# A routed expert kernel: the capacity search spread over twelve tiles with its steps as numbers, and the list scatters five a tile for eight tiles

## The chip, the cores and the metric

The kernel runs on one core of one Trainium2 chip. The metric is the device time of one execution in microseconds (us). TensorE multiplies matrices, VectorE, ScalarE and GpSimd compute, SyncE issues loads and stores; each of them works through its own list of instructions in order and waits on semaphores for the others. GpSimd also issues the indirect DMAs (scatters and gathers by a list of row numbers).

## The reference

One layer: image patches are embedded and joined with text tokens (32 sequences of 274 tokens, 192 wide), then attention with 12 heads, then a layer of experts with two sets of four experts each. The change is in the routing of the experts. What matters of it, cut down:

```python
N = h.shape[0]                      # 8768 tokens
capacity = int(N / 4)               # 2192 tokens for each common expert
pc = softmax(h @ Wsc + bsc); pmax_c = max(pc); route_c = argmax(pc)
dropped = rank of the token by -pmax_c among those of its expert >= capacity
common = sum over e of (route_c == e) * ffn(h, W1c[e], b1c[e], W2c[e], b2c[e])
pu = softmax(h @ Wsu + bsu);        route_u = argmax(pu)
unique = sum over e of (route_u == e) * ffn(h, W1u[e], b1u[e], W2u[e], b2u[e])
out = common + dropped * unique     # unique only where the common expert dropped the token
```

`ffn` is 192 to 768, GELU, back to 192.

## The kernel before, in words

The attention part ends near 830 us. It has written each token's row to `rows_d`, and GpSimd has scattered the rows into `sorted_d`, ordered by common expert. The expert part then works on tiles of 256 rows of one expert. The first 35 (`FIXED`) are common ones, read from `sorted_d`. The later ones belong to the unique experts: their rows are found by lists in `list_d`, which can be made only once it is known which tokens are dropped. Tiles 0 to 43 are written out one by one, the rest sit in a loop that stops at the last tile in use.

Each engine runs `body(t)` for the tiles in turn. For tile t:

- SyncE loads weights and rows four tiles ahead into one of four buffers (`load_w`, `load_sorted`): the big part of the weights at L1547, the rows at L1560, the rest of the weights at L1550. It does so once Y of tile t-4 is done, and for the rows also once GpSimd has read that tile's row numbers out of the buffer (`sid_ready`, waited for at L1558).
- TensorE (`up`, `turn`, `down`): 30 up products for tile t (L1790), four transposes of tile t+1's rows (L1772, L1773), 24 down products of tile t-1 in two halves (L1801).
- ScalarE: GELU for the six blocks of tile t, and rounded copies (`Wh`, `XH`) of the next tile's weights and rows.
- VectorE: the differences `Wl` (L1947, two halves) and `XL`, `XH` (L1938, L1940) of the next tile; then bias (`Yb`, L1957) and sum (`Y`, L1971) of tile t-1.
- GpSimd (a turn of its body): the two row scatters of Y of tile t-3 (`send`, L1690), the copy of tile t-2's row numbers (`number`, the cast `sid` at L1662), and the list scatters where there are any (`send_ids`, L184).

**The search.** A common expert drops the tokens whose `pmax` lies under a threshold. The threshold T of each of the four experts is found by bisection in 26 tests. `test` (VectorE) adds the step to T (`cand`, L1983), compares all keys with it (`flag`, L1984) and sums over a partition (`part`, L1985). `count` (TensorE, L1814) sums over partitions. `take` (VectorE) turns the count into 0 or the step (`gain`, L1989), halves the step (L1990) and adds the gain to T (L1991). The first two (`LEAD`) run ahead of tile 0, where the kernel still waits for loads. The others are spread over the tiles so that each count stands between TensorE's products: `SEARCH` tiles with `TESTS` tests each. `done` makes VectorE wait for each of its own results before the next instruction.

**After it.** `ties` runs in tile `TIES`, `drops` in `DROPS`, `drop_flags` in the next one, `unique_rows` in `PLACE` (it sets `ranked`), `unique_tiles` and `unique_turns` in the two after (which set `placed`; SyncE waits for that in tile `EARLY` = 22). From tile `SPREAD` on GpSimd scatters the 72 columns of token numbers into the lists, so many a tile as the table `BEFORE` says, until tile 31.

**The barrier.** In tile 32 SyncE waits for all of the list scatters before it loads the first list, and everything that it loads afterwards, the weights and rows of tile 33 first, is queued behind this wait:

```python
if t.number == FIXED - AHEAD:
    sp.wait_ge(spread_out, 16 * COLS)
if t.number is not None and FIXED <= t.number + AHEAD < STATIC:
    load_list(...)
```

In the trace this wait is shown at L1571.

Of the kernel before, what the change touches and what calls it, by code (L numbers as in the profile page):

```python
# [10 lines left out]
ALU = mybir.AluOpType  # L11
# [3 lines left out]
P = 128  # L15
# [20 lines left out]
CAP = N // NX  # L36
# [6 lines left out]
FIXED = -(-N // ROWS)  # L43
# [1363 lines left out]
UNITS = GROUP * (NG - 1)  # L1407
AHEAD = 3
STATIC = (-(-CT // DEPTH) + 1) * DEPTH
LEAD, SEARCH, TESTS = 2, 8, 3  # L1410
LOWEST = 0.25 - 2.0 ** -10
TIES, DROPS, PLACE = SEARCH, SEARCH + 1, SEARCH + 3
SPREAD = PLACE + 1
BEFORE = [sum(4 if n < SPREAD + 12 else 3 for n in range(SPREAD, t)) for t in range(FIXED - 2)]
assert (FIXED, CT, STATIC) == (35, 38, 44)
assert LEAD + SEARCH * TESTS >= 26 and BEFORE[-1] >= COLS

# [21 lines left out]
def experts(nc, block, sem, H, A, K, rows_d, sorted_d, list_d, out):  # L1439

    ctx = ExitStack()
    with ctx:
# [9 lines left out]
        C, eye, OH, key = K.c, K.ident, K.OH, K.key  # L1452
        T = sb("T", [P, NX])
        cand = sb("cand", [P, NX])
        step = sb("step", [P, 1])
        gain = sb("gain", [P, NX])
        part = sb("part", [P, NX])
        need = sb("need", [P, NX])
# [302 lines left out]
        def _(pe):  # L1761
# [54 lines left out]
            def body(t):  # L1816
                searching = t.number is not None and t.number < SEARCH
                if t.opens:
                    turn(t)
                up(t)  # L1820
                if searching:
                    count(LEAD + TESTS * t.n)
                if not t.closes:
                    turn(t.next())
                if not t.opens:
                    down(t.before(1), 0)
                if searching:
                    count(LEAD + TESTS * t.n + 1)
                if not t.opens:
                    down(t.before(1), 1)  # L1830
                if searching:
                    count(LEAD + TESTS * t.n + 2)
                if t.number == DROPS:
                    count(LEAD + TESTS * SEARCH)
                    ranks(0, tie96[:].rearrange("p e c -> p (e c)"), NX * FLAT)
                if t.number == DROPS + 1:
                    ranks(1, OH[:, 1].rearrange("p e c -> p (e c)"), NX * COLS)
# [54 lines left out]
        def _(dve):  # L1892
# [21 lines left out]
                done(dve.tensor_tensor_scan(first[:, 0:ne], C["one"][:, 0:ne], K.nt[:, 0:ne], 0.0, ALU.mult, ALU.add))  # L1914

            dve.wait_ge(H.left, 1)
            for x, value in ((T, LOWEST), (step, 0.5)):
                done(dve.memset(x[:], value))

            def by_batch(x):  # L1920
                return x.rearrange("p e (b k) -> p (e b) k", k=3)
# [56 lines left out]
                add_bias(t)  # L1978
                add_rest(t)

            def test():

                done(dve.tensor_scalar(cand[:], T[:], step[:, 0:1], None, ALU.add))  # L1983
                done(dve.tensor_tensor(flag[:], key[:], by_e(cand[:]), ALU.is_ge))  # L1984
                dve.tensor_reduce(part[:], flag[:], AX.X, ALU.add).then_inc(part_ready, 1)  # L1985

            def take(k):
                dve.wait_ge(counted, k + 1)
                done(dve.tensor_scalar(gain[:], cnt_ps, float(CAP), step[:, 0:1], ALU.is_ge, ALU.mult))  # L1989
                dve.tensor_scalar(step[:], step[:], 0.5, None, ALU.mult)  # L1990
                done(dve.tensor_tensor(T[:], T[:], gain[:], ALU.add))  # L1991

            def ties():
# [72 lines left out]
            def body(t):  # L2066
                searching = t.number is not None and t.number < SEARCH
                if t.opens:
                    split(t, 0)
                    split(t, 1)  # L2070
                    turned(t)
                if t.number is not None and 0 < t.number <= SEARCH:
                    take(LEAD + TESTS * t.n - 1)
                if searching:
                    test()
                if not t.closes:
                    split(t.next(), 0)
                if searching:
                    take(LEAD + TESTS * t.n)
                    test()  # L2080
                if t.number == DROPS + 1:
                    drop_flags()
                if t.number == PLACE:
                    unique_rows()
                if t.number == PLACE + 1:
                    unique_tiles()
                if t.number == PLACE + 2:
                    unique_turns()
                if not t.closes:
                    turned(t.next())  # L2090
                if searching:
                    take(LEAD + TESTS * t.n + 1)
                    test()
                if not t.closes:
                    split(t.next(), 1)
                if not t.opens:
                    add_bias(t.before(1))
                    if not t.before(1).based():
                        add_rest(t.before(1))
                    if t.number in (FIXED + 1, CT, CT + 2):  # L2100
                        add_rest(static({FIXED + 1: FIXED, CT: CT - 2, CT + 2: CT - 1}[t.number]))
                    if t.number in (CT + 4, CT + 5):
                        add_rest(static(2 * t.number - CT - 8))
                        add_rest(static(2 * t.number - CT - 7))
                if t.number == TIES:
                    ties()
                if t.number == DROPS:
                    drops()
                if t.number == PLACE:
                    unique_counts()  # L2110

            for k in range(LEAD):
                test()
                take(k)
            tiles(dve, body, load_last, finish)

# [92 lines left out]
```

## Time and profile before

| | |
|---|---|
| median of three runs | 1244.79 us (1237.87 to 1248.96) |
| the profiled execution | 1241.2 us, its span 1239.3 us |
| busy in the span | TensorE 1145.1 us (92%), VectorE 858.9 (69%), ScalarE 607.8 (49%), GpSimd 726.8 (59%) |
| mean granted clock of TensorE | 0.958 of full speed |

The span is what the trace covers, the 1.9 us beside it lie around it. Times in the rows below count from the span's start. A granted clock of 1.00 is TensorE's higher level of 2.4 GHz, 0.50 the lower of 1.2 GHz. The expert part runs from 833 us to the end; the shares of the whole span say little on it, so the rows go by stretch, by tile and by engine. In a line of the timeline the number in brackets is the time in which the engine sat idle before it, and behind the arrow stands what ended it; "issue" is time in which it waited for nothing that the trace shows.

### The profile page before, as it was taken

How to read it: one execution, taken by the hardware profiler on the slowest of the kernel's cores; microseconds unless marked ns; L12 is line 12 of the kernel's file. 1: busy time of each engine (PE TensorE's matmuls, PEld its weight loads, DVE VectorE, ACT ScalarE, POOL GpSimd, SP SyncE). 2: the span in 40 equal slices, each digit the busy share in tenths (PEclk: the TensorE clock that was granted, in tenths of full speed). 3: DMA queues.
4: the chain of work that ended last, by engine and by line, in shares of the span. 5: the costliest groups of instructions: out<-in, count | busy, mean ns of one | idle time of the engine just before them, and what ended most of it. 6: DMA issues, size and time to landing. Idle time of an engine off the chain costs nothing. (4 is left out here: it accounts for less than half of the span.)

```text
span 1239.3 us, 33362 instructions
## 1 busy us (share of the span) xinstructions
PE 1145.1 (92%) x12686; PEld 988.4 (80%) x12686; DVE 858.9 (69%) x1933; ACT 607.8 (49%) x1088; POOL 726.8 (59%) x1126
## 2 busy tenths in 40 slices
PE   4889999999999999999999998737999999999993
PEld 3667888888888788788788786527999999999993
DVE  6557777788788788788788787456988655555341
ACT  2135555555555555555555545414545555555540
POOL 6235555555765765765765763553633877755575
PEclk9879999999999999999999999767999999999997
DMA  6001112113323323322422312258876888978651
GB/s 217 18 23 58 50 43 73 59 44 103 112 69 94 117 74 88 122 75 77 127 81 75 120 65 63 98 164 321 295 261 207 263 270 268 289 223 291 217 179 33
DMA packets 84514, 168.08 MB, mean 136 GB/s; under 512 B 16590, under 2 KB 57845, under 8 KB 84352
## 3 DMA queue, kind: packets, MB, share of 16 engines
q1 hardware_dynamic: 70688, 139.90, 35.8%
q0 software_dynamic: 13664, 26.00, 5.9%
q8 instruction: 104, 1.70, 0.6%
q14 instruction: 58, 0.48, 0.1%
HBM read 123.85 MB, written 45.45 MB: 137 GB/s over the span
## 5 line engine op out<-in xcount | busy, mean ns | idle before, releaser
L811 ACT ACTIVATE PT<-round_banks 128x1752 f32<-128x1752 f32 x96 | 156.7, 1632 | 110.4 <-PE round_banks L632 110.4
L1880 ACT ACTIVATE Gl<-h_ps,W 128x256 f32<-128x256 f32 x264 | 115.9, 474 | 169.6 <-PE h_ps L1790 161.2
L958 POOL TENSOR_SCALAR_AFFINE_SELECT PT<-PT 128x512 f32<-128x512 f32 x192 | 118.3, 643 | 114.6 <-ACT PT L811 114.1
L1801 PE MATMUL y_ps<-W,Gl 128*128 128x192 f32 x1056 | 181.2, 325 | 0.0
L1801 PEld LDWEIGHTS y_ps<-W,Gl 128*128 128x128 f32 x1056 | 171.3, 189 | 0.0
L1790 PE MATMUL h_ps<-XH,Wh 128*128 128x256 f32 x528 | 147.5, 297 | 6.8 <-issue 2.6
L1790 PE MATMUL h_ps<-XH,Wl 128*128 128x256 f32 x528 | 140.2, 287 | 0.0
L1084 DVE TENSOR_TENSOR capped<-round_banks,masks_f 128x1024 f32<-128x1024 f32 x96 | 117.3, 1222 | 31.6 <-PE round_banks L605 31.6
L533 PE MATMUL gen<-w_emb,xh 128*128 128x192 f32 (+1 forms) x768 | 125.1, 270 | 14.0 <-POOL xl L898 13.7
L1690 POOL DMA_INDIRECT out_dram<-Y,sid x76 | 79.6, 1048 | 77.7 <-DVE Y L1971 56.7
L1947 DVE TENSOR_TENSOR Wl<-W,Wh 128x768 fp32r<-128x768 f32 x88 | 84.3, 959 | 56.8 <-ACT Wh L1860 54.3
L533 PEld LDWEIGHTS gen<-w_emb,xh 128*128 128x128 f32 (+1 forms) x768 | 102.9, 168 | 19.8 <-issue 15.4
L632 PEld LDWEIGHTS round_banks<-QKT 32*128 32x128 f32 x2304 | 95.2, 188 | 27.8 <-issue 14.5
L1088 DVE TENSOR_REDUCE nm<-capped 128x8 f32<-128x1024 f32 x96 | 116.0, 1208 | 0.0
L632 PE MATMUL round_banks<-QKT 32*128 32x146 f32 (+2 forms) x2304 | 110.0, 319 | 5.3 <-DMA QKT<-mT 2.4
L1790 PEld LDWEIGHTS h_ps<-XH,Wh 128*128 128x128 f32 x528 | 103.2, 195 | 8.5 <-DVE Wl L1947 5.8
L918 POOL TENSOR_SCALAR veps<-mv 128x2 f32<-128x2 f32 (+1 forms) x80 | 18.0, 225 | 151.8 <-DVE mv L1096 150.5
L1790 PEld LDWEIGHTS h_ps<-XH,Wl 128*128 128x128 f32 x528 | 103.2, 196 | 0.0
L533 PE MATMUL gen<-w_emb,xl 128*69 128x192 f32 (+1 forms) x384 | 101.8, 265 | 0.0
L605 PEld LDWEIGHTS round_banks<-QKT 32*128 32x128 f32 x1536 | 71.4, 189 | 37.2 <-issue 26.7
L235 POOL DMA_INDIRECT sorted_d<-stage,pos x72 | 74.3, 1032 | 41.2 <-DMA stage<-rows_d 19.8
L605 PE MATMUL round_banks<-QKT 32*128 32x256 f32 (+1 forms) x1536 | 92.7, 356 | 5.5 <-ACT PT L811 5.3
(287 smaller groups left out, 2662.0 us busy)
## 6 DMA issues: line engine op xcount, KB each, us to landing
W<-in_experts_dram SPq DMA_DIRECT2D x44, 771.0 KB, 5.4
W<-in_experts_dram SPq DMA_DIRECT2D x44, 672.0 KB
xT<-in_xT_dram SPq DMA_DIRECT2D x32, 591.0 KB, 4.8
X<-sorted_d SPq DMA_DIRECT2D x35, 386.0 KB, 5.7
stage<-rows_d SPq DMA_DIRECT2D x64, 192.0 KB
rows_d<-h SPq DMA_DIRECT2D x32, 192.0 KB, 3.9
out_dram<-h SPq DMA_DIRECT2D x32, 192.0 KB, 6.5
rows_d<-xn SPq DMA_DIRECT2D x32, 192.0 KB, 2.1
```

The source lines that it names most:

```text
L533: mm = pe.matmul(g[0:m, 0:D], x[:, c, cols], w_emb[:, c, part_of_w, :], start=(c == 0 and n == 0), stop=(c == EC - 1 and n == 2))
L605: mm = pe.matmul(R[:, i, at:at + (k + 1) * P], q[rows, j, tok(k)], q[rows, JG + j, 0:(k + 1) * P], start=True, stop=True, skip_group_check ...
L632: mm = pe.matmul(R[:, i, at:at + n], q[rows, JG + j, klo:klo + P], q[rows, j, qlo:qlo + n], start=True, stop=True, skip_group_check=True)
L811: act.activation(PT[(JG * b + j) % 2][:], R[:, :, 0:438], ACT.Exp, scale=SCALE).then_inc(exps, 1)
L958: pool.affine_select(x[:, :, at:at + P], x[:, :, at:at + P], [[0, GH], [1, P]], ALU.is_ge, 0.0, base=0, channel_multiplier=-1)
L1084: dve.tensor_tensor(capped[:], blocks[:, :, 0:3:2, :], masks[:].rearrange("p (a b k) -> p a b k", a=1, b=1).broadcast_to([P, GH, 2, P]), A ...
L1088: dve.tensor_reduce(x[:, :, 0:3:2], capped[:], AX.X, ALU.max, negate=True).then_inc(capped_read, 1)
L1690: pool.indirect_dma_start(out_rows, bass.IndirectOffsetOnAxis(target(t)[:, k:k + 1], 0), Y[t.i][:, k, :], None, bounds_check=N - 1, oob_is ...
L1790: mm = pe.matmul(h_ps[f % 3][:, 0:ROWS], w[t.par][:, cols], x, start=(k == 0), stop=(k == len(products) - 1))
L1801: mm = pe.matmul(y_ps[t.par][:, k * D:(k + 1) * D], Gl[t.par][:, f, k * P:(k + 1) * P], W[t.i][:, W2O + f * D:W2O + (f + 1) * D], start=(f ...
L1880: act.activation(Gl[t.par][:, f, :], h_ps[f % 3][:, 0:ROWS], ACT.Gelu, bias=W[t.i][:, B1O + f:B1O + f + 1]).then_inc(g_ready, 1)
L1947: dve.tensor_tensor(halves(Wl[t.par], half), halves(W[t.i], half), halves(Wh[t.par], half), ALU.subtract).then_inc(wl_ready, 1)
```

## The change

The search takes twelve tiles with two tests each in place of eight with three. The step of each test is written into the instructions as a number (a power of a half), so the tile `step`, its memset and its halving (L1990) are gone, and `cand` and `gain` have no second input of a column. All that follows the search moves four tiles on, by the names that are set from `SEARCH`: the ties from tile 8 to 12, the drops from 9 to 13, `unique_rows` from 11 to 15. The list scatters start in tile 16 in place of 12; they were four a tile for twelve tiles and three for eight, and are now five a tile for eight tiles and four for eight.

```diff
-LEAD, SEARCH, TESTS = 2, 8, 3
+LEAD, SEARCH, TESTS = 2, 12, 2
-BEFORE = [sum(4 if n < SPREAD + 12 else 3 for n in range(SPREAD, t)) for t in range(FIXED - 2)]
+BEFORE = [sum(5 if n < SPREAD + 8 else 4 for n in range(SPREAD, t)) for t in range(FIXED - 2)]
...
-        step = sb("step", [P, 1])
...
-                if searching:
-                    count(LEAD + TESTS * t.n + 2)
...
-            for x, value in ((T, LOWEST), (step, 0.5)):
-                done(dve.memset(x[:], value))
+            done(dve.memset(T[:], LOWEST))
...
-            def test():
-
-                done(dve.tensor_scalar(cand[:], T[:], step[:, 0:1], None, ALU.add))
+            def test(k):
+
+
+                done(dve.tensor_scalar(cand[:], T[:], 0.5 ** (k + 1), None, ALU.add))
...
-                done(dve.tensor_scalar(gain[:], cnt_ps, float(CAP), step[:, 0:1], ALU.is_ge, ALU.mult))
-                dve.tensor_scalar(step[:], step[:], 0.5, None, ALU.mult)
+                done(dve.tensor_scalar(gain[:], cnt_ps, float(CAP), 0.5 ** (k + 1), ALU.is_ge, ALU.mult))
...
                 if searching:
-                    test()
+                    test(LEAD + TESTS * t.n)
...
                     take(LEAD + TESTS * t.n)
-                    test()
+                    test(LEAD + TESTS * t.n + 1)
...
-                if searching:
-                    take(LEAD + TESTS * t.n + 1)
-                    test()
```

How it moves instructions, at two places. On VectorE in one search tile, from the test before the first half of `Wl` to the next tile's bias, before:

```order
L1983 TENSOR_SCALAR cand<-T,step 128x4
L1984 TENSOR_TENSOR flag<-key,cand 128x288
L1985 TENSOR_REDUCE part<-flag 128x4
L1947 TENSOR_TENSOR Wl<-W,Wh 128x2x384
...
L1938 TENSOR_TENSOR XL<-xt_ps,XH 128x256
L1940 TENSOR_TENSOR XH<-xt_ps,XH 64x256
L1989 TENSOR_SCALAR gain<-in_col_ps,step 128x4
L1990 TENSOR_SCALAR step<-step 128x1
L1991 TENSOR_TENSOR T<-T,gain 128x4
L1983 TENSOR_SCALAR cand<-T,step 128x4
L1984 TENSOR_TENSOR flag<-key,cand 128x288
L1985 TENSOR_REDUCE part<-flag 128x4
L1947 TENSOR_TENSOR Wl<-W,Wh 128x2x384
```

And now:

```order
L1980 TENSOR_SCALAR cand<-T 128x4
L1981 TENSOR_TENSOR flag<-key,cand 128x288
L1982 TENSOR_REDUCE part<-flag 128x4
L1943 TENSOR_TENSOR Wl<-W,Wh 128x2x384
L1986 TENSOR_SCALAR gain<-in_col_ps 128x4
L1987 TENSOR_TENSOR T<-T,gain 128x4
L1980 TENSOR_SCALAR cand<-T 128x4
L1981 TENSOR_TENSOR flag<-key,cand 128x288
L1982 TENSOR_REDUCE part<-flag 128x4
L1934 TENSOR_TENSOR XL<-xt_ps,XH 128x256
L1936 TENSOR_TENSOR XH<-xt_ps,XH 64x256
L1943 TENSOR_TENSOR Wl<-W,Wh 128x2x384
```

The take and the test between `XH` and the second half of `Wl` are gone, and the halving of the step with every other take. On GpSimd where the lists are scattered, the turns of tiles 23 and 24 before, each with two row scatters (of `Y`, to the rows in `sid`), a cast and its lists:

```order
L1690 DMA out_0_dram<-Y0,sid0 8768x192 x2
L1662 CAST sid1<-X1 128x2
L184 DMA list_d<-meta,pos 39168x2 x4
L1690 DMA out_0_dram<-Y1,sid1 8768x192 x2
L1662 CAST sid2<-X2 128x2
L184 DMA list_d<-meta,pos 39168x2 x3
```

The same turns now:

```order
L1689 DMA out_0_dram<-Y0,sid0 8768x192 x2
L1661 CAST sid1<-X1 128x2
L184 DMA list_d<-meta,pos 39168x2 x5
L1689 DMA out_0_dram<-Y1,sid1 8768x192 x2
L1661 CAST sid2<-X2 128x2
L184 DMA list_d<-meta,pos 39168x2 x4
```

Each turn from tile 16 to 31 has one list scatter more than it had, the turns of tiles 12 to 15 have none.

## Rows read from the trace of the kernel before

**Rows 1.** Busy time by stretch, us; x counts instructions, PEclk is the granted clock.

```profile
core 0: us, PE busy (x) PEld busy (x) DVE busy (x) ACT busy (x) POOL busy (x), PEclk, DMA share, GB/s
852.00:854.00 2.00, 0.48 (x3) 0.48 (x3) 1.90 (x6) 0.00 (x0) 0.00 (x0) 0.50 0.99 402
858.00:860.00 2.00, 2.00 (x18) 2.00 (x18) 1.12 (x2) 1.88 (x5) 0.40 (x1) 0.93 0.64 215
910.25:919.29 9.04, 8.96 (x66) 8.52 (x66) 8.47 (x26) 4.58 (x9) 2.76 (x3) 1.00 0.67 229
972.39:980.33 7.94, 7.94 (x60) 7.94 (x60) 4.14 (x8) 4.51 (x9) 6.41 (x7) 1.00 0.91 260
1051.80:1115.36 63.56, 63.56 (x466) 63.56 (x466) 32.66 (x56) 36.13 (x72) 42.27 (x50) 1.00 0.83 261
```

**Rows 2.** Waits of SyncE's queue from 860 to 1140: us, times, longest.

```profile
SPq L1571 <- DMA list_d<-meta,pos: 8.1, 1, 8.1
SPq L1559 <- POOL sid L1662: 1.6, 1, 1.6
```

**Rows 3.** Timeline at the list barrier: start, us, engine, instruction.

```profile
1113.95 0.34 SPq L1547 DMA_DIRECT2D W<-in_experts_dram  x1
1119.56 0.33 PE L1772 MATMUL xt_ps<-ident,X 128*128 128x128 f32 x1 [0.31 <-DMA X<-sorted_d]
```

**Rows 4.** Timeline of VectorE in tiles 0, 7 and 10.

```profile
851.28 0.43 DVE L1940 TENSOR_TENSOR XH<-xt_ps,XH 64x256 fp32r<-64x256 f32 x1
917.27 0.22 DVE L1989 TENSOR_SCALAR gain<-in_col_ps,step 128x4 f32<-128x4 f32 x1
917.78 0.23 DVE L1983 TENSOR_SCALAR cand<-T,step 128x4 f32<-128x4 f32 x1
918.54 0.45 DVE L1985 TENSOR_REDUCE part<-flag 128x4 f32<-128x288 f32 x1
937.05 0.16 DVE L2007 TENSOR_SCALAR need<-in_col_ps 128x4 f32<-128x4 f32 x1
```

**Rows 5.** Timeline of TensorE in tiles 0, 1, 4 and 7.

```profile
853.52 0.59 PE L1814 MATMUL in_col_ps<-part,ones 128*128 128x4 f32 x2 [2.14 <-DVE part L1985]
853.97 0.56 PE L1790 MATMUL h_ps<-XH,Wh 128*128 128x256 f32 x1
891.94 0.39 PE L1814 MATMUL in_col_ps<-part,ones 128*128 128x4 f32 x2
916.77 2.21 PE L1801 MATMUL y_ps<-W,Gl 128*128 128x192 f32 x12
919.05 0.39 PE L1814 MATMUL in_col_ps<-part,ones 128*128 128x4 f32 x2
```

**Rows 6.** Timeline of SyncE: two loads of sorted rows.

```profile
878.86 0.34 SPq L1560 DMA_DIRECT2D X<-sorted_d  x1
984.02 0.34 SPq L1560 DMA_DIRECT2D X<-sorted_d  x1
```

**Rows 7.** DMA issues from 860 to 900: count, KB each, median us to landing.

```profile
X<-sorted_d SPq DMA_DIRECT2D x4, 386.0 KB, 6.3
```

**Rows 8.** The list scatters: ns min/median/max, first and last start.

```profile
L184 POOL DMA_INDIRECT list_d<-meta,pos x72: 972/975/1708, 955.2 to 1107.7; - x72
```

**Rows 9.** Timeline of GpSimd: turns of tiles 15, 16 and 24.

```profile
977.86 0.98 POOL L1690 DMA_INDIRECT out_dram<-Y,sid  x1 [0.30 <-issue]
980.48 0.98 POOL L184 DMA_INDIRECT list_d<-meta,pos  x1 [0.16 <-POOL sid L1662]
985.80 0.97 POOL L1690 DMA_INDIRECT out_dram<-Y,sid  x1 [0.30 <-issue]
1049.35 0.97 POOL L1690 DMA_INDIRECT out_dram<-Y,sid  x1 [0.31 <-issue]
```

**Rows 10.** Timeline of VectorE and GpSimd where a list scatter is longest.

```profile
964.43 0.96 DVE L1947 TENSOR_TENSOR Wl<-W,Wh 128x768 fp32r<-128x768 f32 x1
964.53 1.71 POOL L184 DMA_INDIRECT list_d<-meta,pos  x1 [0.30 <-issue]
```

More of the change, by code:

```diff
@@ L2112, in _ @@
             for k in range(LEAD):
-                test()
+                test(k)
                 take(k)
```

## The prediction

> **What bounds the kernel now.** I read the busy time by stretch first [rows 1]. The change touches only the expert part, from 833 us on. In the tile from 972.39 to 980.33 and again from 1051.80 to 1115.36 TensorE is busy in all of the stretch at a granted clock of 1.00: an expert tile costs TensorE 7.94 us, and nothing else sets the pace. Two kinds of stretch differ. A search tile (910.25 to 919.29) takes 9.04 us, and VectorE is busy 8.47 of them. At the start of the part TensorE does little: 0.48 of 2 us from 852 to 854, with its clock at 0.50.
>
> Then the waits of SyncE's queue: it stood 8.1 us at L1571 until the last list scatter had landed [rows 2]. That looks harmless, since TensorE waited only 0.31 us for the rows that SyncE loads behind this barrier (tile 33's transposes at 1119.56 [rows 3]). But a wait above zero means that the barrier has no slack left: whatever makes the last list scatter later makes the end later. So GpSimd's chain of scatters has to be timed beside TensorE's tiles.
>
> **Part 1, the search.** In a search tile VectorE takes a count (gain 0.22 us, with the step's and T's updates the next test starts 0.51 after it at 917.78), and makes the next test, whose part takes 0.45 and ends at 918.99, three times [rows 4]. A take and a test are 1.7 us, from 917.27. On TensorE the third count started at 919.05, after down products that began at 916.77 and, 12 at 0.158 (a tile's 24 take 3.78), would have ended at 918.66: 0.39 us of waiting, and 0.24 until the next tile started at 919.29 [rows 1, 5]. With two tests a tile VectorE has 9.04 - 1.7 = 7.3 us to do. Steps as numbers save more: L2007, two numbers on the same PSUM tile, took 0.16 where gain took 0.22 [rows 4]; with as much on cand and 0.07 for the step's own multiply, 0.2 a test, it is 6.9 us. That is under TensorE's 7.94, so TensorE sets the search tiles: 7.94 + two counts of 0.14 to 0.24 = 8.3 us (8.45 if the second test is late by 0.15).
>
> Tiles 5 to 7 gain 3 x (9.04 - 8.3) = 2.2 us. Tiles 8 to 11 now carry two counts each, 4 x 0.35 = 1.4 us lost. The tie, drop and place steps keep their price, four tiles later, and `placed` still comes before tile 22, where SyncE asks for it.
>
> At the start, the third test of tile 0 held TensorE: 2.14 us idle ahead of its count, and tile 1 started at 853.97 [rows 5]. Without it tile 1 starts when XH ends, at 851.7 [rows 4], 2.2 us earlier, perhaps at the higher clock too. It won't keep this: tile 5's rows were issued only at 878.86 [rows 6], 1.6 us behind their time for a sid cast on GpSimd [rows 2], and the search doesn't move that cast, which stands behind the last staged scatters. They take 6.3 us to land in this stretch [rows 7], until 885.2; transposes, down products and a count take 4.45 more; tile 5 starts at 889.6. Today the count ahead of it begins at 891.94 [rows 5], so it starts at 892.3: 2.7 us won, between 1.5 (rows land later) and 5 (they are not waited for).
>
> Part 1 alone: 2.7 + 2.2 - 1.4 = **3.5 us faster**, if GpSimd keeps up. What VectorE loses besides is hidden by TensorE's tile; that cover is 1 us.
>
> **Part 2, the list scatters.** The 72 of them started from 955.2 to 1107.7, 0.975 us each with 0.30 before the next [rows 8, 9]. A turn of GpSimd at four lists is two row scatters and the sid cast (977.86 to 980.48, 2.62 us) and 4 x 1.28 for the lists: 7.74 us; the next began at 985.80. From 977.86 to 1049.35 nine turns took 71.49 us, 7.94 each [rows 9]. GpSimd is full there already, with 0.2 us a turn for stretches. At five lists a turn is 9.02 us, 1.1 more than TensorE's tile, and in the last eight tiles four lists (7.74) stand where three did. GpSimd becomes the slowest engine for sixteen tiles.
>
> So I time it as a chain that waits for nobody: 71 list starts after the first (90.9 us) and 15 turns' other work at 2.62 (39.3): 130.2 us. Today 19 turns lie between (140.7 us) and it takes 152.5, with room for 11.8 of waits and stretches. Stretches: a scatter that starts while VectorE's Wl runs gets longer; the longest, 1.71 for 0.98 us, began 0.10 after a Wl of 0.96 [rows 10]. The first stretch of turns, beside the place steps, took 977.86 - 955.20 = 22.66 for 12 lists and two turns' rest (20.6): 2.06 over. Low bound: 2.06 + 13 turns x 0.2 = 4.7 us. High: the longest stretch once a turn, 2.06 + 13 x 0.73 = 11.6. I take 5.5, near the steady turns.
>
> The first list is at 955.2 now, in tile 12; then in tile 16: 955.2 - 2.7 - 2.2 + 4 x 8.3 = 983.5. The last: 983.5 + 130.2 + 5.5 = 1119.2, **11.5 us later** than 1107.7. From the last list to the next weights' issue are 6.28 us (to 1113.95 [rows 3]), and TensorE was already waiting behind those. So the 11.5 go to the end whole, and part 1's gain is inside them, since it only starts the chain earlier. Queued behind the barrier on SyncE are the weights and rows of tile 33 and of all later ones. Before that, late sid casts hold back the rows of tiles 23 to 26: today the cast ends just before 980.48 for rows that are issued at 984.02 [rows 6, 9], 3.5 us of room, gone after three or four turns at 1.1. Those small stalls lie inside the same 11.5.
>
> The long one is in one piece. Tile 32 can start some 12.6 us after turn 30 (cast 2.6, rows 5.7, transposes and down products 4.3), at 1117, and its up products end at 1121; tile 33's rows land at 1119.2 + 6.3 + 5.6 = 1131.1. Ten us idle, and the clock was at 0.50 after far less (852 to 854), and at 0.93 in the stretch from 858 to 860, 4 to 5 us after tile 1 had started [rows 1, 5]. Half speed for 4.3 us costs 2.2 us, between 0 (clock kept) and 2.5. "TensorE: Matmul & The Clock Gate" of the Trainium skill (part "What's actually happening") names the same two levels, 1.2 and 2.4 GHz; by that rule, the trace agrees.
>
> **The sum.** 11.5 + 2.2 = 13.7 us. The profiled execution took 1241.2 us, 1.9 over its span; with 13.7 it is 1254.9. It lies 3.6 under the median of the three runs, 1244.79, which becomes **1258.5**. Bounds: the chain with 4.7, tile 5 at 887.3 and no clock loss, 1116.1 - 1107.7 = 8 us, 1253. The chain with 11.6, tile 5 at 890.8, clock 2.5: 18.8 + 2.5 = 21, 1266.
>
> **Rivals.** (a) GpSimd has room: the 0.30 us ahead of each scatter is put down to issue and not to work, so five might be issued closer. The lists then end in time, only part 1 counts, and the time is 1244.8 - 3.5 = 1241, not slower. It decides from a spacing under 1.12 us (11.5 us less over 71 starts). Against it: nine turns in a row held 1.28. "DMA: Bandwidth & Descriptors" of the Trainium skill (section "Anatomy of one DMA — SWDGE (gpsimd) path") calls descriptor generation small and puts most of the fixed 2 us of a DMA at its completion; by that, a fifth scatter is nearly free to GpSimd and the time is that of (a). The trace doesn't agree: GpSimd is busy 0.97 us with each.
>
> (b) The delay is partly swallowed: after the barrier the loads come closer together, or the last tiles, where VectorE waits for base rows anyway, absorb it. Half stays, some 6 us: 1251. Against it: those waits start from the Y of tiles behind the barrier, which move too. (c) GpSimd is stretched as in the high bound or more, as it no longer runs in step with the tiles: 1266 to 1270. "SBUF — State Buffer" of the Trainium skill (section "Who interferes with whom") says that a VectorE instruction with two SBUF inputs contends with a GpSimd one that reads SBUF, and the first blocks the other; the row at 964.53 agrees.
>
> **How the numbers follow.** The forecast (8 to 17 us slower) has 0.68, (a) 0.12, (b) 0.10, (c) 0.10. Within 1%, 12.4 us, a measurement of this kernel can't tell a change from none. That cuts the forecast in two: 0.38 of its 0.68 lie above, and with (c) slower has 0.48. Faster by over 1% would need three times part 1: 0.03, taken from (a). The rest, 0.49, is within. The range takes in the bounds and most of (b), and leaves out (a) and the far end of (c): 1246 to 1266.
>
> **What would show it.** Search tiles of 8.3 us with VectorE idle in them; gain near 0.16 us; turns of 9.0 to 9.5 us on GpSimd in tiles 17 to 23, none waiting for Y; SyncE waiting for sid casts from tile 23 on; the last list near 1119; TensorE idle some 10 us ahead of tile 33's transposes, a clock of 0.50 behind it. It is wrong if GpSimd still waits for Y in tiles 24 to 31, or if TensorE's wait at tile 33 stays under 1 us.

## The result, and the profile after

The changed kernel takes **1262.99 us** (median of 4 runs, 1256.93 to 1263.42), the kernel before 1241.56 (median of 4, 1237.87 to 1248.96). The ratio is 1.0132 with a 95% interval of 1.0099 to 1.0165: 16.4 us slower, between 12.3 and 20.5. The forecast was 1258.5 and 13.7 us slower.

The profiled execution took 1262.94 us, with a span of 1261.2 against 1239.3 before, 21.9 us more. Not all of that is the change's. The first count on TensorE, with which the expert part begins, stands at 838.39 us here and at 834.03 before, and ahead of it the change touches only VectorE's memset and its first `cand`. Over the twelve kernels profiled for this study, it stands anywhere from 830.24 to 840.97. So below I measure from the first count. From there to the end of the span are **405.3 us before and 422.8 after: 17.5 us more**.

The search did what was expected. First the busy time by stretch, as in [rows 1]: a search tile, the tile-4 wait, and the stretch around tile 33.

```profile
core 0: us, PE busy (x) PEld busy (x) DVE busy (x) ACT busy (x) POOL busy (x), PEclk, DMA share, GB/s
921.00:929.34 8.34, 8.34 (x64) 8.34 (x63) 6.61 (x17) 4.58 (x9) 2.44 (x3) 1.00 0.71 232
877.00:880.00 3.00, 0.26 (x4) 0.17 (x2) 0.00 (x0) 0.00 (x1) 2.33 (x3) 0.96 0.90 295
880.00:883.00 3.00, 1.88 (x8) 1.88 (x9) 1.99 (x6) 2.66 (x6) 2.53 (x4) 0.50 1.01 418
...
1127.00:1131.00 4.00, 1.00 (x9) 0.79 (x7) 0.00 (x0) 0.00 (x0) 2.92 (x3) 1.00 0.08 21
1133.00:1137.00 4.00, 0.00 (x0) 0.00 (x0) 0.71 (x1) 1.58 (x4) 3.09 (x4) 0.50 1.00 322
1137.00:1141.00 4.00, 3.88 (x14) 3.88 (x15) 2.06 (x4) 1.68 (x3) 1.75 (x3) 0.50 1.02 403
```

In the search tile TensorE is busy in all 8.34 us and VectorE in 6.61 of them (8.47 of 9.04 before [rows 1]). A take and a test on VectorE, as in [rows 4]:

```profile
925.86 0.15 DVE L1986 TENSOR_SCALAR gain<-in_col_ps 128x4 f32<-128x4 f32 x1
926.05 0.16 DVE L1987 TENSOR_TENSOR T<-T,gain 128x4 f32<-128x4 f32 x1
926.25 0.17 DVE L1980 TENSOR_SCALAR cand<-T 128x4 f32<-128x4 f32 x1
```

The steps as numbers made gain 0.15 us where it was 0.22, and cand 0.17 where it was 0.23. cand starts 0.39 after gain, not 0.51.

GpSimd and SyncE, as in [rows 2, 8, 9]: the scatters of the lists, one turn of five lists from start to start, and what SyncE's queue waited for from 860 to 1140.

```profile
L184 POOL DMA_INDIRECT list_d<-meta,pos x72: 971/974/1715, 991.0 to 1127.1; - x72
```

```profile
1008.50 0.97 POOL L1689 DMA_INDIRECT out_dram<-Y,sid  x1 [0.30 <-issue]
...
1011.11 0.98 POOL L184 DMA_INDIRECT list_d<-meta,pos  x1 [0.16 <-POOL sid L1661]
...
1017.72 0.97 POOL L1689 DMA_INDIRECT out_dram<-Y,sid  x1 [0.30 <-issue]
```

```profile
SPq L1558 <- POOL sid L1661: 54.0, 14, 5.7
SPq L1570 <- DMA list_d<-meta,pos: 12.3, 1, 12.3
```

The turn takes 9.22 us, against TensorE's tile of 7.94; after a first one of 10.6 beside the place steps, six turns of five lists took 9.0 to 9.6. The 72 lists run in 136.1 us without a wait for `Y`. SyncE now stands at the sid cast in 14 tiles (one before), for up to 5.7 us, and 12.3 us at the barrier.

What it ends in, as in [rows 3]: SyncE's first loads behind the barrier, and TensorE at tile 33.

```profile
1131.05 0.34 SPq L1546 DMA_DIRECT2D W<-in_experts_dram  x1
1132.15 0.34 SPq L1559 DMA_DIRECT2D X<-sorted_d  x1
...
1137.12 0.48 PE L1771 MATMUL xt_ps<-ident,X 128*128 128x128 f32 x1 [9.13 <-DMA X<-sorted_d]
```

TensorE waits **9.13 us** where it waited 0.31 before. The transpose itself takes 0.48 and not 0.27 to 0.33, since the clock is at 0.50. From there to the next `Yb` on VectorE, the sum that follows a tile's down products and so marks the start of the next tile, are 7.33 us, 4.68 before.

The chain of waits runs straight through this. Its pieces from 1124 us on:

```profile
1124.52 0.97 POOL list_d L184
1125.80 0.99 POOL list_d L184
1127.09 2.09 DMA list_d<-meta,pos
1132.15 4.93 DMA X<-sorted_d
1137.12 0.48 PE xt_ps L1771
1138.24 6.10 PE y_ps L1800 x24
```

Ahead of the barrier it is GpSimd that stands on the chain. In a stretch that TensorE bounds there would be rows of `h_ps` and `y_ps`.

One thing went otherwise than predicted, at the start. TensorE in tile 4:

```profile
881.12 0.47 PE L1771 MATMUL xt_ps<-ident,X 128*128 128x128 f32 x1 [3.86 <-DMA X<-sorted_d]
```

It arrived earlier than before, waited 3.86 us for tile 4's rows, and the clock fell to 0.50 (the row of 880 to 883 above). Before, there was no wait there:

```profile
877.50 0.31 PE L1772 MATMUL xt_ps<-ident,X 128*128 128x128 f32 x1
```

**Where the 17.5 us are.** I follow the starts of the tiles (by their `Yb`) and the last list, each from its kernel's first count. At tile 5 the changed kernel is 0.2 us ahead, at tile 18 0.1. The last list comes at 288.7 instead of 273.6: 15.1 later. From there to the landing of tile 33's rows are 10.03 us (1137.12 - 1127.09) instead of 11.89: 1.9 won. From the transposes to `Yb` are 2.65 more, the clock. What follows takes 116.7 us instead of 115.1: 1.6 more. Together 15.1 - 1.9 + 2.65 + 1.6 = 17.5. The last term is within what this stretch varies by: it took from 112.6 to 118.7 us in eleven of the twelve kernels profiled (in fill4_barrier33 a wait for rows lies inside it).

### The profile page after: what moved, and what is told of

The parts are those of the page before. It is cut to its first block and busy times, and to the rows that moved or that the text cites. A ratio compares the mean times of both kernels' runs of the same rounds, so it can differ in the third digit from the quotient of the medians.

```text
span 1261.2 us, 33335 instructions
## 1 busy us (share of the span) xinstructions
PE 1152.9 (91%) x12686; PEld 997.3 (79%) x12686; DVE 853.7 (68%) x1906; ACT 608.2 (48%) x1088; POOL 727.7 (58%) x1126
## 5 line engine op out<-in xcount | busy, mean ns | idle before, releaser
L1800 PE MATMUL y_ps<-W,Gl 128*128 128x192 f32 x1056 | 186.3, 331 | 0.0
L1800 PEld LDWEIGHTS y_ps<-W,Gl 128*128 128x128 f32 x1056 | 175.6, 193 | 0.0
L533 PE MATMUL gen<-w_emb,xh 128*128 128x192 f32 (+1 forms) x768 | 128.2, 275 | 14.0 <-POOL xl L898 13.7
L550 PE MATMUL gen<-w_qkv,xnT 97*128 97x200 f32 (+1 forms) x256 | 96.8, 461 | 1.6 <-ACT xnT L789 1.6
```

The lines of the kernel that those rows point to most:

```text
L533: mm = pe.matmul(g[0:m, 0:D], x[:, c, cols], w_emb[:, c, part_of_w, :], start=(c == 0 and n == 0), stop=(c == EC - 1 and n == 2))
L550: pe.matmul(o, xTs[:, 0, tok(k)], w[0:KC + 1, 0, cols], start=True, stop=False)
L1800: mm = pe.matmul(y_ps[t.par][:, k * D:(k + 1) * D], Gl[t.par][:, f, k * P:(k + 1) * P], W[t.i][:, W2O + f * D:W2O + (f + 1) * D], start=(f ...
```

## The experiments

All ratios are against the kernel before, run beside it on the same chip. "Profiled" is the time of the one profiled execution; in some kernels it lies far from the median, and what is read from its rows need not hold for the others. "Part" is the time from the first count to the end of the span, "last list" the start of the last list scatter from the first count, both of that execution; "tile 4" and "barrier" are what TensorE waited for rows there, us.

| kernel | median us | profiled | ratio (95%) | part | last list | tile 4 | barrier |
|---|---|---|---|---|---|---|---|
| before | - | 1241.20 | 1 | 405.3 | 273.6 | - | 0.31 |
| after | 1262.99 | 1262.94 | 1.0132 (1.0099 to 1.0165) | 422.8 | 288.7 | 3.86 | 9.13 |
| steps_only | 1240.61 | 1240.35 | 0.9976 (0.9945 to 1.0006) | 404.4 | 271.5 | 0.49 | 0.34 |
| late_lists | 1258.46 | 1254.78 | 1.012 (1.008 to 1.0161) | 422.3 | 288.5 | - | 9.17 |
| half_lists | 1240.55 | 1234.90 | 0.9971 (0.9943 to 1.0) | 400.7 | 269.8 | 2.68 | - |
| barrier33 | 1246.88 | 1240.11 | 1.003 (1.0003 to 1.0058) | 408.1 | 286.8 | 3.13 | - |
| lead4 | 1249.07 | 1250.66 | 1.0064 (1.004 to 1.0088) | 407.8 | 279.7 | 1.19 | 6.87 |
| filled_wait | 1258.23 | 1247.96 | 1.014 (1.0108 to 1.0173) | 415.8 | 288.7 | 3.79 | 0.17 |
| lead6_barrier33 | 1240.62 | 1239.85 | 0.9993 (0.9964 to 1.0021) | 407.7 | 276.7 | - | - |
| steps_barrier33 | 1240.09 | 1242.42 | 0.9972 (0.9946 to 0.9997) | 402.6 | 271.3 | - | - |
| fill4_barrier33 | 1246.87 | 1254.16 | 1.0021 (0.9985 to 1.0058) | 415.4 | 286.0 | 0.82 | 4.25 |
| lead4_barrier33 | 1240.97 | 1240.18 | 0.9962 (0.9931 to 0.9994) | 404.4 | 282.5 | 3.25 | 0.57 |

**steps_only**: the kernel before, with three tests a tile and its lists where they were, and only the steps written as numbers.

```diff
-                done(dve.tensor_scalar(cand[:], T[:], step[:, 0:1], None, ALU.add))
+                done(dve.tensor_scalar(cand[:], T[:], 0.5 ** (k + 1), None, ALU.add))
...
-                done(dve.tensor_scalar(gain[:], cnt_ps, float(CAP), step[:, 0:1], ALU.is_ge, ALU.mult))
-                dve.tensor_scalar(step[:], step[:], 0.5, None, ALU.mult)
+                done(dve.tensor_scalar(gain[:], cnt_ps, float(CAP), 0.5 ** (k + 1), ALU.is_ge, ALU.mult))
```

> The kernel before with the steps as numbers alone; search of eight tiles with three tests, lists as before. Theory 1 (list chain and barrier make the loss): a search tile falls from 9.04 to about 8.6 us on VectorE, some 0.45 us in each of eight tiles, so 3 to 4 us faster than before if the list chain keeps its room; the last list stays about 152 us behind the first. Theory 2 (the searching tiles themselves carry the loss, whatever GpSimd does): nothing of it is in this kernel, also 0 to 4 us faster. What it tells: the size of this part alone.

Search tiles take 8.45 to 8.58 us instead of 8.90 to 9.04, with all three tests in them, and the last list comes 2.1 us earlier. In the part 0.9 us is left of it. The ratio's interval takes in 1: a gain of up to 7 us or none. So most of what the cheaper search brings needs neither fewer tests a tile nor later lists: three tests with numbers cost 8.5 us, two cost 8.34.

**late_lists**: the kernel before, with its own search, and the changed kernel's plan for the lists alone.

```diff
-SPREAD = PLACE + 1
-BEFORE = [sum(4 if n < SPREAD + 12 else 3 for n in range(SPREAD, t)) for t in range(FIXED - 2)]
+SPREAD = PLACE + 5
+BEFORE = [sum(5 if n < SPREAD + 8 else 4 for n in range(SPREAD, t)) for t in range(FIXED - 2)]
```

> The kernel before with its search as it was, and only the list scatters moved: they start in tile 16 and go five a tile for eight tiles and four for eight. Theory 1: first list near 985, last 135.5 to 136 us behind it, near 1121, 13 us later than before; TensorE idle 9 to 10 us ahead of tile 33's transposes, clock 0.50 behind it; 13 to 16 us slower than before. Theory 2: as fast as before.

This is the whole loss by itself: 1.012 against the change's 1.0132, and a part of 422.3 against 422.8. The lists of late_lists, and TensorE at tile 33:

```profile
L184 POOL DMA_INDIRECT list_d<-meta,pos x72: 971/972/1578, 984.0 to 1119.1; - x72
```

```profile
1129.23 0.48 PE L1772 MATMUL xt_ps<-ident,X 128*128 128x128 f32 x1 [9.17 <-DMA X<-sorted_d]
```

They are in the same place from the first count as in the changed kernel (288.5 and 288.7), although this kernel's search is the slow one: the first list comes 0.7 us later here, the chain behind it is 0.9 shorter. So the changed kernel's search is worth next to nothing there. In this execution tile 5 started 1.5 us later than before (60.2 from the first count, not 58.7): at the end of tile 3 TensorE waited 2.02 us for a `part` (0.82 before), and in tile 4 the clock stood at 0.50 for 3.4 us. Without that the lists would presumably have ended a little earlier.

**half_lists**: the changed kernel with only 36 of the 72 list scatters; the other half of the lists is left out, and the late tiles gather fewer rows.

```diff
-                        sp.wait_ge(spread_out, 16 * COLS)
+                        sp.wait_ge(spread_out, 16 * COLS // 2)
...
-                    for c in range(min(BEFORE[t.number], COLS), min(BEFORE[t.number + 1], COLS)):
+                    for c in range(min(BEFORE[t.number] // 2, COLS // 2), min(BEFORE[t.number + 1] // 2, COLS // 2)):
```

> The changed kernel with only 36 of the 72 list scatters (the other half of the lists stays empty, so the late tiles gather fewer rows), search of twelve tiles with two tests. Theory 1: no turn of GpSimd is longer than a tile, no wait of TensorE at tile 33; the search costs nothing or little against before: between 4 us faster and 3 us slower. Theory 2: 10 to 16 us slower than before, like the changed kernel.

With turns that have room, the last list comes at 269.8, TensorE waits for nothing at the barrier, and the time is 0.9971 of before. That is some 20 us under the changed kernel's. All of its loss needs GpSimd to be full: where its turns have room, the later start of the lists costs nothing. The fewer rows of the late tiles could help too, but the stretch from tile 33 to the end took 113.4 us here, inside what the kernels with all lists show.

**barrier33**: the changed kernel, with SyncE's wait for the last list, and the list loads behind it, one tile later.

```diff
-                    if t.number == FIXED - AHEAD:
+                    if t.number == FIXED - AHEAD + 1:
 
                         sp.wait_ge(spread_out, 16 * COLS)
-                    if t.number is not None and FIXED <= t.number + AHEAD < STATIC:
-                        load_list(Tile((t.number + AHEAD) // DEPTH, (t.number + AHEAD) % DEPTH))
+                    if t.number is not None and FIXED <= t.number + AHEAD - 1 < STATIC:
+                        load_list(Tile((t.number + AHEAD - 1) // DEPTH, (t.number + AHEAD - 1) % DEPTH))
```

> The changed kernel with the wait for the list scatters, and every list load, one tile later on SyncE, behind the loads of tile 33. The same work. Theory 1: tile 33's weights and rows no longer stand behind the barrier, those of tile 34 do; the last list lands as late as before, but TensorE waits 1 to 3 us in place of 9 and keeps its clock: 8 to 11 us faster than the changed kernel, 3 to 8 us slower than the kernel before. Theory 2: no change against the changed kernel, 16 us slower than before.

The lists end nearly as late as in the change (286.8 for 288.7), yet the part is 408.1 and the ratio 1.003: about four fifths of the loss are gone by one position of one wait. (This part is that of the fastest of twelve executions; by the ratios 0.0132 falls to 0.003.) What SyncE's queue waited for in this kernel, from 860 to 1140:

```profile
SPq L1558 <- POOL sid L1661: 50.4, 16, 5.8
...
SPq L1570 <- DMA list_d<-meta,pos: 5.2, 1, 5.2
```

The waits for sid casts are all still there, and cost little beyond two tiles (`Yb` 9.65 and 12.40 us apart there, 6.2 above two normal tiles). The 3.7 us that this part is longer than that of steps_only are within that.

**lead4**: four tests ahead of the tiles, eleven search tiles; so lists one tile earlier, five a tile in four tiles and then four.

```diff
-LEAD, SEARCH, TESTS = 2, 12, 2
+LEAD, SEARCH, TESTS = 4, 11, 2
...
-BEFORE = [sum(5 if n < SPREAD + 8 else 4 for n in range(SPREAD, t)) for t in range(FIXED - 2)]
+BEFORE = [sum(5 if n < SPREAD + 4 else 4 for n in range(SPREAD, t)) for t in range(FIXED - 2)]
```

> The changed kernel with four tests ahead of tile 0 and eleven search tiles of two, so the lists start in tile 15 and go five a tile for four tiles and four for thirteen. Lengths are counted from the first count on TensorE to the end of the span, since the part before differs from one execution to the next (405.3 us for the kernel before, 422.8 for the changed one). Theory 1 (the chain of 71 list starts at 1.28 and the other work of each turn at 2.62, plus some 5.5 us, runs from the first list to the last and then to the barrier): first list 8.3 us earlier than in the changed kernel, one turn more in the chain, so the last is 5.5 to 6 us earlier and the part 416 to 418 us. The two more tests ahead of tile 0 cost nothing, since TensorE waits there for rows, and again ahead of tile 4. Theory 2 (what counts is the number of lists in a turn, four or five): with only four turns of five, nearly all of the loss is gone, 407 to 410.

The last list comes 9.0 us earlier than in the change (5.5 to 6 were expected), and the ratio falls from 1.0132 to 1.0064, some 8 us. The chain itself is as theory 1 has it, 138.3 us for 136.1 and one turn more of 2.6. The part, 407.8, is where theory 2 had it, but the lists are only 9.0 of its 15.0: 0.7 are the rows landing sooner behind the last list, 1.1 the clock, and 4.1 the stretch behind tile 33, which varies as much from kernel to kernel without any such cause. There is a second thing in the start. TensorE at tile 4, and the clock around it, in lead4:

```profile
883.43 0.33 PE L1771 MATMUL xt_ps<-ident,X 128*128 128x128 f32 x1 [1.19 <-DMA X<-sorted_d]
```

```profile
core 0: us, PE busy (x) PEld busy (x) DVE busy (x) ACT busy (x) POOL busy (x), PEclk, DMA share, GB/s
...
880.00:883.00 3.00, 2.24 (x20) 2.15 (x18) 1.24 (x4) 1.20 (x3) 2.08 (x4) 1.00 0.99 336
883.00:886.00 3.00, 2.57 (x18) 2.47 (x18) 2.47 (x7) 2.67 (x6) 2.53 (x4) 1.00 1.00 407
```

Tile 4's rows land 42.5 us after the first count, as in the change (42.7). But the tiles ahead of it began two tests later, so TensorE waits 1.19 and not 3.86, and the clock stays at 1.00. Tile 5 starts at 55.7 from the first count here, at 58.5 in the change, at 58.7 before. The kernel that started its tiles later reached tile 5 first.

**filled_wait**: the changed kernel with eleven products of constants added on TensorE ahead of tile 33's transposes.

```diff
+                if t.number == FIXED - AHEAD:
+                    for _ in range(11):
+                        pe.matmul(in_col[:, 0:NX * FLAT], K.before[:], tie96[:].rearrange("p e c -> p (e c)"), start=True, stop=True)
```

> The changed kernel with eleven products of 128x384 on TensorE (results not used) between tile 32's up products and the transposes of tile 33, about 8.3 us in the 9.1 us that it waits there. Theory 1: the clock stays at 1.00 over the wait, tile 31's down products take 3.9 us in place of 6.1, and the kernel is 2 to 2.5 us faster than the changed kernel (part of 420 to 421 us). If the clock costs nothing on the path, or the products are late themselves: no change or slower.

TensorE in filled_wait, from the added products on:

```profile
1121.39 7.26 PE L1824 MATMUL in_col_ps<-tie,before 128*128 128x384 f32 x22
1128.81 0.33 PE L1771 MATMUL xt_ps<-ident,X 128*128 128x128 f32 x1 [0.17 <-DMA X<-sorted_d]
```

The rows land 9.73 us after the last list (10.03 in the change), so the products only fill the wait, and the clock stays at 1.00. From transposes to `Yb` are 4.69 us, as before the change (4.68), not 7.33. So the clock's share is 2.65 us. The ratio (1.014) doesn't show it: its interval and the change's lie on each other. By time this experiment is inconclusive, by its rows it is not. Its part of 415.8 is no measure either: the profiled execution was the fastest of six, 10.3 us under their median, and 4.1 us of the difference to the change lie behind tile 33.

**lead6_barrier33** and **steps_barrier33**: six tests ahead, ten search tiles and four lists a tile, and the later barrier; and the kernel before with steps as numbers and the later barrier. Their edits beyond those shown:

```diff
-LEAD, SEARCH, TESTS = 2, 12, 2
+LEAD, SEARCH, TESTS = 6, 10, 2
...
-BEFORE = [sum(5 if n < SPREAD + 8 else 4 for n in range(SPREAD, t)) for t in range(FIXED - 2)]
+BEFORE = [sum(4 for n in range(SPREAD, t)) for t in range(FIXED - 2)]
```

> Six tests ahead of tile 0, ten search tiles of two, lists four a tile in tiles 14 to 31, and the list barrier behind tile 33's loads. Theory 1: first list 14 to 17 us earlier than in the changed kernel; no turn of GpSimd longer than a tile, the last list 12 us earlier than in the changed kernel and no wait of note ahead of tiles 33 and 34. Part of 400 to 403 us, 2 to 5 us faster than the kernel before. If the four more tests ahead of tile 0 are not hidden (9 us of them against 4.4 us of waiting at tile 0 and 3.9 at tile 4), 1 to 4 us of that are lost. Theory 2: the barrier's place doesn't matter and the early tests count in full: slower than before by 3 us or more.

> The kernel before with the steps as numbers and the list barrier behind tile 33's loads, search and lists else as before. Theory 1: the part falls from 404.4 (steps as numbers alone) by the 0.5 us that tile 33 waited, to some 404 us: 1 us faster than before. A gain of 3 us or more would show that the barrier cost more than its own wait.

Neither waits at tile 4 or at the barrier. lead6_barrier33 keeps four lists a tile, and SyncE waits 0.9 us in all for sid casts (54.0 in the change). But with its four more tests ahead of the tiles it reaches tile 5 at 59.0, no sooner than the kernel before (58.7), and the time is that of before: 0.9993. Its part, 407.7 where 400 to 403 were expected, also has the longest stretch behind tile 33, 118.7 us. steps_barrier33 has the shortest median, 0.9972 (0.9946 to 0.9997), and can't be told from steps_only: with the lists as before the barrier had no cost to be taken away.

**fill4_barrier33**: barrier33 with 26 added transposes of constants ahead of tile 4's.

```diff
+                if t.number == 4:
+                    pe.wait_ge(xt_ready, t.n)
+                    for _ in range(26):
+                        pe.transpose(xt_ps[:, 0:P], K.before[:], eye[:])
```

> The changed kernel with the list barrier one tile later, and with 26 added transposes of constants (128x128, the same form as the tile's own) on TensorE ahead of tile 4's transposes, written where the real ones overwrite them. They stand in the 3.1 us in which TensorE waited for tile 4's rows; nothing is left out. Theory 1, the start's gain is lost to the clock that falls while TensorE waits for tile 4's rows: at full clock the fillers take some 2.9 us, the wait behind them is under 0.5, the clock stays at 1.00 from there on, and the interval of the base rows' sums over tile 4 goes from 13.0 to some 10.3 us; the part is some 2.7 us shorter than with the late barrier alone (408.1 from the first count), the time 1244. Rival, the rows' landing alone sets tile 5, whatever the clock does: the interval stays near 13, the time 1247.

TensorE at tile 4 in fill4_barrier33:

```profile
875.34 3.04 PE L1766 MATMUL xt_ps<-ident,before 128*128 128x128 f32 x26
879.20 0.33 PE L1775 MATMUL xt_ps<-ident,X 128*128 128x128 f32 x1 [0.82 <-DMA X<-sorted_d]
```

The rows land at 42.25 from the first count, about as ever (42.7 in the change), and the clock stays at 1.00. From transposes to `Yb` are 4.9 us, where they are 7.5 in the change, in filled_wait and in lead4_barrier33. Tile 5 starts at 55.5, 3.2 earlier than before the change and 3.1 earlier than in it: 2.6 the clock, the rest the rows. So the clock does bear on tile 5, and the rival, that the rows' landing alone sets it, falls. The time didn't follow: 1246.87, as with the late barrier alone (1246.88). Against that kernel tile 5 starts only 0.9 us sooner (56.4 there), too little for these times to show. In the profiled execution, the slowest of eleven at 1254.16, it was lost again by a wait for the barrier in tile 34:

```profile
1136.02 0.47 PE L1775 MATMUL xt_ps<-ident,X 128*128 128x128 f32 x1 [4.25 <-DMA X<-sorted_d]
```

Whether the executions near the median wait there too isn't shown. In this one the step from the last list to the next weights' issue took 6.14 us, in barrier33 4.70.

The interval of 10.3 us that I expected was 12.29. I had taken the whole 2.7 off barrier33's 13.0, and in barrier33 the clock was back after 6.2 us and had cost only 1.3; the rows also landed 0.4 later.

**lead4_barrier33**: lead4 with the later barrier.

> Four tests ahead of the tiles and eleven search tiles, lists five a tile for four tiles and then four, with the list barrier one tile later on SyncE. The earlier tiles start two tests (some 2.6 us) later and the rows of tile 4 are waited for only 1.2 us, so the clock should stay at 1.00. Theory 1: no stall of TensorE over 1 us at tile 33 and none over 2 at tile 4; the part takes some 403 to 405 us from the first count, the time 1241 to 1244, 5 to 8 below the four-tests kernel with the early barrier (1249.07). Rival, the last list at some 1120 minus the attention part's spread is still too late for tile 34: a wait of 1 to 3 us there, the time 1245.

1240.97 us, 0.9962 (0.9931 to 0.9994), with 0.57 us of waiting at the barrier: the time that was expected. But in this execution the early tiles ran faster (tile 2 starts at 27.3 from the first count, in lead4 at 29.3), TensorE waited 3.25 for tile 4's rows, and the clock fell to 0.50. So four tests ahead do not protect tile 4; lead4's profile showed one outcome of two. The low ratio is the late barrier with fewer turns of five lists. The lowest ratios of kernels that do all the work, 0.9962, 0.9972 and 0.9976, can't be told apart.

## Why the prediction was right, and where its terms were off

**Part 1, the search: right.** Search tiles 8.34 us for a forecast of 8.3, gain 0.15 for 0.16, VectorE idle in them. Tiles 5 to 7 gain 1.9 us of the 2.2, and tiles 8 to 11 lose 1.6 for 1.4.

**Part 1, the start: the mis-sized term.** "So it starts at 892.3: 2.7 us won", in bounds of 1.5 to 5, measured 0.2. I asked where the rows of tile 5 would hold TensorE, and passed over tile 4's, which land 42 us after the first count whatever the search does. Before, the slow search covered them with no wait at all. Without it TensorE waits 3.86 us, and the clock falls, which costs 2.6 more. In fill4_barrier33, which keeps the clock, the start does win 3.2. So the first list, forecast for 149.5 us after the first count, came at 152.6: 2.5 of the 3.1 are the start, the rest the search tiles.

**Part 2, the chain: right.** 136.1 us from first list to last, forecast 135.7; late_lists shows 135.2 and barrier33 136.4. Turns of 9.0 to 9.6 were forecast as 9.0 to 9.5. The model "GpSimd waits for nobody, add its turns" held because nothing in tiles 17 to 31 let it wait. The last list came 15.1 us later for a forecast of 11.5; the 3.6 are the first list's 3.1 and the chain's 0.4.

**The barrier: right in place, a little off in size.** The step "from the last list to the next weights' issue are 6.28 us" was taken over unchanged, and measured 3.96 (1131.05 - 1127.09). In filled_wait, late_lists and lead4 it is 3.96 or 3.97. What goes with it is the traffic: in these four executions the DMA engines stood at 0.02 of their time in the 2 us from the last list's start, since the loads had been held up. In the three with the early barrier and no wait of note (before, steps_only and half_lists) they stood at 0.98 to 1.02, and the step took 6.28, 6.50 and 6.63. No run took the traffic alone away, so that it is the cause is argued. The wait of 9.13 us was forecast as ten.

**The clock: right, low.** 2.65 us for a forecast of 2.2 (at most 2.5). Half speed lasted 5.4 us, over the transposes and nearly all of the down products (4.3 were forecast); the clock was back at 1.00 by 1143 us, ahead of tile 33's up products at 1144.0.

**The rivals.** (a), room on GpSimd, is refuted: list scatters start 1.28 us apart in turns of five as in turns of four. The rule of the Trainium skill that stood beside it ("DMA: Bandwidth & Descriptors", section "Anatomy of one DMA — SWDGE (gpsimd) path") calls descriptor generation small; for these scatters the trace doesn't agree, GpSimd is busy 0.97 us in each. (b), half swallowed, was right in one thing: 1.9 us come back as the loads behind the barrier land sooner. In the tail, behind tile 33, I had argued that the waits move along. VectorE waits there twice for base rows. The second wait, in the changed kernel, lead6_barrier33, lead4 and barrier33:

```profile
1201.04 0.75 DVE L1967 SCALAR_TENSOR_TENSOR Y<-Yb,late_X,base_rows 128x192 f32<-128x192 f32 x2 [7.69 <-DMA base_rows<-out_dram,sid]
```

```profile
1176.76 0.75 DVE L1967 SCALAR_TENSOR_TENSOR Y<-Yb,late_X,base_rows 128x192 f32<-128x192 f32 x2 [8.20 <-DMA base_rows<-out_dram,sid]
```

```profile
1187.04 0.75 DVE L1967 SCALAR_TENSOR_TENSOR Y<-Yb,late_X,base_rows 128x192 f32<-128x192 f32 x2 [1.45 <-DMA base_rows<-out_dram,sid]
```

```profile
1176.47 0.75 DVE L1967 SCALAR_TENSOR_TENSOR Y<-Yb,late_X,base_rows 128x192 f32<-128x192 f32 x2 [1.43 <-DMA base_rows<-out_dram,sid]
```

The kernels fall into two groups here. In eight, the kernel before among them, this wait is 7.3 to 8.2 us, in four it is 1.2 to 1.5. It doesn't go with the barrier: of the kernels with no wait of note there, lead6_barrier33 has the long one and barrier33 the short one, and of those with a long wait there, the change has the long one and lead4 the short one. From tile 33's `Yb` to the end are 116.7 us in the change, 115.1 before, 112.6 in lead4 and filled_wait, 118.7 in lead6_barrier33. So no run shows that the tail swallows any of a delay; it differs by up to 6.1 us between the profiled executions, whatever came before it. Ahead of the 7.69 us GpSimd had stood 5.40 us until a row scatter had landed, in lead4 1.52. Why it lands early or late stays open. (c), stretched scatters, is not what happened: the longest is 1715 ns (1708 before), and the chain is 5.9 us over its bare turns. The time came out above the forecast for other reasons, the start above all.

**The size is partly luck.** From forecast to profile the terms moved by 3.6 (the last list), -1.9 (the landing), 0.45 (the clock) and 1.6 (the tail): 13.7 became 17.5. One of the four has the other sign, and by the ratio, 16.4 in 12.3 to 20.5, the forecast can't be told from the measurement.

**The change does what it says**, and its two parts undo each other by construction. Twelve search tiles push the lists four tiles later. The lists then need turns of 9.2 us beside tiles of 7.94. So GpSimd sets the end. What is won ahead of the first list reaches the end only by starting the chain earlier, and what is won between the first list and the last doesn't reach it.

## What to carry to other kernels

When work moves, add up the full turn of the engine that takes it, and compare it with the tile of the engine that sets the pace. Over it, that engine is a chain of its own, which can be summed row by row and here was, to 0.4 us in 136. A barrier with a wait of 0.31 us behind it has no slack: look what is queued behind it and whether it could stand one tile later, which here brought back four fifths of the loss. To start earlier is only a gain if the next load is there; earlier arrival at a wait can end in a lower clock and give nearly all of it back.

## What the runs showed of the hardware

- **A wait's second price.** From tile 4 on, TensorE's clock stood at its lower level, 0.50, in or behind ten waits for rows of 2.56 to 9.17 us (in eight executions), and this cost 1.3 to 2.65 us on top of the wait. Fifteen others, of 0.49 us or more, kept it at 1.00, the longest of them 2.29 and 2.62 us. So the length of the wait alone doesn't decide, as the two kernels below show (their next `Yb` came 6.35 and 4.68 us later). In late_lists the clock also fell behind a wait of 2.02 us for a `part`, not for rows. Added products in the wait kept it at 1.00 at both places.

TensorE at tile 26's rows, in barrier33 (the clock at 0.50 behind it) and in fill4_barrier33 (at 1.00):

```profile
1062.02 0.33 PE L1771 MATMUL xt_ps<-ident,X 128*128 128x128 f32 x1 [2.56 <-DMA X<-sorted_d]
```

```profile
1067.50 0.33 PE L1775 MATMUL xt_ps<-ident,X 128*128 128x128 f32 x1 [2.62 <-DMA X<-sorted_d]
```

- **Operand as a number.** A TENSOR_SCALAR of 128x4 on VectorE took 0.15 us with the step as a number where it took 0.22 with the step in a tile (from PSUM), and 0.17 for 0.23 (from SBUF).
- **A quiet memory.** From the start of the last list scatter to SyncE's next weight load, behind the barrier, were 3.96 or 3.97 us in four executions with the DMA engines at 0.02 of their time, and 6.28 to 6.63 in three with them at 0.98 to 1.02.
- **Who starts first.** Of the 828 list scatters of the twelve executions, 164 began while a `Wl` ran on VectorE. The 91 that had 0.28 to 0.88 us of it still before them took over 1.05 us, longer by that rest less some 0.12. Of the other 73, which took 0.97 to 1.05, 72 began in its last 0.1 us and one within 5 ns of its start. None of the 222 scatters during which a `Wl` began was stretched. So which of the two began first decided it, and 0.77 us was the most that it cost.
